# Cross-attention and expert kernel: the softmax probabilities transposed by DMA in f16 halves

## The reference

```
xn      = layernorm(x)
q, k, v = xn @ Wq.T, ctx @ Wk.T, ctx @ Wv.T          (16 heads of 64)
weights = softmax(q k^T / sqrt(128) + bias)          (128 x 120 for each head)
x       = x + (weights @ v) @ Wp.T
y       = layernorm(x)
x       = x + expert_ffn(y)                          (8 experts, top-32 tokens each in 128)
```

## Time and profile before

| | |
|---|---|
| time, median of 3 runs | 1197.02 us (1196.4 to 1198.01) |
| span of the profiled execution | 1194.1 us; the median lies 2.9 us above it |
| PE busy, by the page | 1133.8 us (95%) |
| ACT busy | 1010.4 us (85%) |
| DVE busy | 936.9 us (78%) |
| POOL busy | 663.5 us (56%) |
| attention stage | about 27 to 858 us of the span |
| PE, ACT, DVE, POOL busy from 451.7 to 464.5 us (one slot) | 12.80, 12.56, 11.37, 7.02 us |

### The profile page before, as it was taken

The page is one execution under the profiler, slowest core; times in us unless marked ns, Lnnn a source line. Parts: engine busy times, 40 slices in busy tenths (PEclk is TensorE's granted clock), DMA queues, the critical chain, the costliest instruction groups (busy, mean ns, idle before and its releaser), DMA issues. The chain is left out here.

```text
span 1194.1 us, 50330 instructions
## 1 busy us (share of the span) xinstructions
PE 1133.8 (95%) x15688; PEld 963.1 (81%) x15688; DVE 936.9 (78%) x3847; ACT 1010.4 (85%) x2919; POOL 663.5 (56%) x1149
## 2 busy tenths in 40 slices
PE   3999999999999999999999999999569999999996
PEld 3899999999999999999999999999436666666664
DVE  3888888888888888888888888888685665666553
ACT  3999999999999999999999999999447666666562
POOL 4555555555555555555555555554207767767673
PEclk9999999999999999999999999999869999999998
DMA  3000000000000000000000000000000111111112
GB/s 99 18 18 21 19 15 18 19 15 18 19 15 18 20 15 15 23 15 15 23 15 15 21 17 15 18 19 4 2 1 19 33 48 44 27 53 43 45 54 62
DMA packets 37002, 29.72 MB, mean 25 GB/s; under 512 B 13920, under 2 KB 30304, under 8 KB 36960
## 3 DMA queue, kind: packets, MB, share of 16 engines
q1 hardware_dynamic: 36096, 27.02, 8.6%
q10 hardware_dynamic: 864, 2.16, 0.5%
HBM read 16.58 MB, written 4.19 MB: 17 GB/s over the span
## 5 line engine op out<-in xcount | busy, mean ns | idle before, releaser
L383 ACT ACTIVATE probs<-neg,negmax 128x120 f32<-128x120 f32 x1024 | 322.9, 397 | 2.2 <-DVE negmax L412 0.6
L229 POOL TENSOR_TENSOR v_lo<-v_f,v_hi 120x256 f16<-120x256 f32 x256 | 167.9, 656 | 270.9 <-ACT v_hi L361 152.4
L412 DVE CUSTOM_DVE_ANT_0 neg<-bk_s,bias_sb 128x120 f32<-128x120 f32 x1024 | 228.4, 279 | 88.7 <-PE bk_s L536 80.0
L1101 POOL TENSOR_TENSOR hid<-hid_f,hid 128x512 f16<-128x512 f32 x128 | 167.6, 1313 | 73.7 <-ACT hid L1055 72.8
L422 DVE TENSOR_TENSOR qk_lo<-bk_a,qk_hi 128x496 f16<-128x496 f32 x256 | 171.5, 670 | 7.2 <-ACT qk_hi L346 7.2
L453 DVE TENSOR_TENSOR pT_lo<-bk_t,pT_hi 120x512 f16<-120x512 f32 x256 | 169.9, 664 | 0.3
L545 PE MATMUL bk_t<-ident,probs 128*120 128x128 f32 x1024 | 166.7, 285 | 1.6 <-ACT probs L383 1.6
L346 ACT CAST qk_hi<-bk_a 128x496 f16<-128x496 f32 x256 | 146.6, 572 | 24.6 <-PE bk_a L520 9.7
L375 ACT CAST pT_hi<-bk_t 120x512 f16<-120x512 f32 x256 | 157.5, 615 | 2.4 <-PE bk_t L545 2.4
L621 PE MATMUL bk_y<-wp_sb,oT 128*128 128x128 f32 x1024 | 156.2, 275 | 0.0
L1155 DVE TENSOR_TENSOR hid_f<-bk_u,silu 128x512 f32<-128x512 f32 x128 | 88.3, 690 | 85.4 <-ACT silu L1048 35.0
(11 more groups left out here) (168 smaller groups left out, 3981.7 us busy)
## 6 DMA issues: line engine op xcount, KB each, us to landing
y_all<-y SPq DMA_DIRECT2D x128, 64.0 KB, 2.0
wst<-ffn_w SPq DMA_DIRECT2D x64, 96.0 KB, 1.9
x_sb<-x SPq DMA_DIRECT2D x64, 64.0 KB, 1.8
out<-x_sb SPq DMA_DIRECT2D x16, 256.0 KB, 2.0
ctx_f<-ctx_t SPq DMA_DIRECT2D x64, 60.0 KB, 1.9
w_f<-wqkv_t ACTq DMA_DIRECT2D x3, 512.0 KB, 5.3
wp_sb<-wp_t ACTq DMA_DIRECT2D x1, 512.0 KB, 6.1
bias_sb<-bias ACTq DMA_DIRECT2D x1, 60.0 KB, 6.1
```

The costliest lines, as they stand in the source:

```text
L229: pool.tensor_tensor(v_lo[par][0:K, GH * g:GH * (g + 1), :], v_f[g % 2][0:K, :, :], v_hi[par][0:K, GH * g:GH * (g + 1), 0:DH], ALU.subtrac ...
L383: e = nc.scalar.activation(probs[g % 2][:, i, :], neg[g % 2][:, i, :], ACT.Exp, bias=negmax[g % 2][:, i:i + 1], scale=-1.0)
L412: r = nc.vector.tensor_tensor_reduce(out=neg[g % 2][:, i, :], in0=bk_s[i % 2][:, (i // 2) * K:(i // 2 + 1) * K], in1=bias_sb[:, :], scale= ...
L1101: nc.gpsimd.tensor_tensor(hid[1][par][:, ic, :], hid_f[ic % 2][:, :], hid[0][par][:, ic, :], ALU.subtract).then_inc(hid_lo_ready, 1)
```

## The change

PE makes no transposes of the probabilities any more. POOL casts the f32 probabilities (128 x 4 x 120) to their upper f16 half in the new buffer `p_parts` (128 columns for each head, the last 8 set to zero at the start), DVE subtracts it from the f32 probabilities to get the lower half, and SP issues a transposing DMA for each half, 128 x 512 f16 (128 KB), from SBUF to SBUF, into the new buffer `pT`. There are four buffers of each, one for each group of a slot. The casts of `pT_hi` on ACT and of `pT_lo` from PSUM on DVE go away, and so does the bank `bk_t`. PV runs four groups behind the scores (it was two), the output transposes five (three), the projection six (four). The residual add and its statistics move from step 3 of slot t (batch t-2) to step 1 (batch t-3), the second layernorm from batch t-3 to t-4, and one slot is added at the end (DRAIN 4). SP's three loads of a slot stand between the transposes, on two semaphores in place of one, and x and the context are loaded one slot earlier.

```diff
-DRAIN = 3
+DRAIN = 4
+PV_LAG = 4
+TURN_LAG = PV_LAG + 1
+PROJ_LAG = PV_LAG + 2
...
 @block.sync
+            def turn(t, g):
+                n = 4 * (t - 1) + g
+                for part, ready in ((0, p_hi_ready), (1, p_lo_ready)):
+                    sp.wait_ge(ready, n + 1)
+                    alone(sp)
+                    if part == 0 and some(n - GROUPS + 1):
+                        sp.wait_ge(pv_written, n - GROUPS + 1)
+                        alone(sp)
+                    sp.dma_start_transpose(pT[g][:, part * GH:(part + 1) * GH, :],
+                                           p_parts[g][:, part, :, :].rearrange("p b c -> p (b c)")
+                                           ).then_inc(pT_moved[g], 16)
             def slot(t, par):
...
+                if live(t - 1):
+                    turn(t, 0)
+                if live(t + 2):
+                    load_x(t + 2, par)
+                if live(t - 1):
+                    turn(t, 1)
+                if live(t + 1):
+                    load_ffn(t + 1, (par + 1) % 2)
+                if live(t - 1):
+                    turn(t, 2)
+                    turn(t, 3)
...
 @block.gpsimd
+            for i in range(GROUPS):
+                pool.memset(p_parts[i][:, :, :, K:], 0.0).then_inc(const_ready, 1)
...
+            def upper_parts(t, g):
+                if live(t - 1):
+                    n = 4 * (t - 1) + g
+                    pool.wait_ge(probs_ready, n + 1)
+                    if some(t - 1):
+                        pool.wait_ge(pT_moved[g], 32 * (t - 1))
+                    alone(pool)
+                    pool.tensor_copy(p_parts[g][:, 0, :, 0:K], probs[g % 2][:, :, :]).then_inc(p_hi_ready, 1)
...
+                upper_parts(t - 1, GROUPS - 1)
                 values(t - 1, GROUPS - 1, i)
...
                     pool.tensor_scalar(wsc[:, :], wst[par][:, :], WSCALE, None, ALU.mult).then_inc(pool_chain, 1)
+                upper_parts(t, 0)
                 values(t, 0, par)
...
+                upper_parts(t, 1)
                 values(t, 1, par)
...
+                upper_parts(t, 2)
                 values(t, 2, par)
...
 @block.scalar
-                b1, g1 = behind(t, g, 1)
-                if live(b1):
-
-                    act.wait_ge(pT_written, 4 * b1 + g1 + 1)
-                    if some(4 * b1 + g1 - 1):
-                        act.wait_ge(pv_written, 4 * b1 + g1 - 1)
-                    nc.scalar.copy(pT_hi[g1 % 2][0:K, :, :].rearrange("p a b -> p (a b)"),
-                                   bk_t[0:K, :]).then_inc(pT_hi_ready, 1)
...
 @block.vector
-                    dve.wait_ge(pT_hi_ready, 4 * b1 + g1 + 1)
-                    if some(4 * b1 + g1 - 1):
-                        dve.wait_ge(pv_written, 4 * b1 + g1 - 1)
-                    nc.vector.tensor_tensor(pT_lo[g1 % 2][0:K, :, :].rearrange("p a b -> p (a b)"), bk_t[0:K, :],
-                                            pT_hi[g1 % 2][0:K, :, :].rearrange("p a b -> p (a b)"),
-                                            ALU.subtract).then_inc(pT_lo_ready, 1)
+                    dve.wait_ge(p_hi_ready, 4 * b1 + g1 + 1)
+                    nc.vector.tensor_tensor(p_parts[g1][:, 1, :, 0:K], probs[g1 % 2][:, :, :],
+                                            p_parts[g1][:, 0, :, 0:K], ALU.subtract).then_inc(p_lo_ready, 1)
...
-                if g == GROUPS - 1 and live(t - 2):
-
-                    dve.wait_ge(proj_written, 4 * (t - 2) + 4)
-                    nc.vector.tensor_tensor(x_sb[:, t - 2, :], x_sb[:, t - 2, :], bk_y[:, 0:D],
+                if g == (PROJ_LAG + 3) % GROUPS and live(t - 3):
+
+                    dve.wait_ge(proj_written, 4 * (t - 3) + 4)
+                    nc.vector.tensor_tensor(x_sb[:, t - 3, :], x_sb[:, t - 3, :], bk_y[:, 0:D],
                                             ALU.add).then_inc(x1_ready, 1)
...
 @block.tensor
-                b1, g1 = behind(t, g, 1)
-                if live(b1):
-                    pe.wait_ge(probs_ready, 4 * b1 + g1 + 1)
-                    if some(4 * b1 + g1):
-                        pe.wait_ge(pT_lo_ready, 4 * b1 + g1)
-                    for i in range(GH):
-                        m = nc.tensor.transpose(bk_t[0:K, i * S:(i + 1) * S], probs[g1 % 2][:, i, :], ident[:, :])
-                    m.then_inc(pT_written, 1)
-                b2, g2 = behind(t, g, 2)
+                b2, g2 = behind(t, g, PV_LAG)
                 if live(b2):
 
-                    p2 = (par + 1) % 2 if g >= 2 else par
-                    pe.wait_ge(pT_lo_ready, 4 * b2 + g2 + 1)
+                    p2 = par
+                    pe.wait_ge(pT_moved[g2], 32 * (b2 + 1))
```

More of the change, by code:

```diff
@@ L118, in attention @@
         probs = two("probs", [S, GH, K], F32)
-        pT_hi = two("pT_hi", [128, GH, S], F16)
-        pT_lo = two("pT_lo", [128, GH, S], F16)
+        p_parts = [sb(f"p_parts{i}", [S, 2, GH, 128], F16) for i in range(GROUPS)]
+        pT = [sb(f"pT{i}", [128, 2 * GH, S], F16) for i in range(GROUPS)]
         rsum = sb("rsum", [S, GH], F32)
@@ L205, in _, with load_x, load_ffn @@
-            slots(sp, slot, end=B, first=0)
+            def load_x(b, par):
+                if some(b):
+                    sp.wait_ge(loaded_xc, 32 * b)
+                    alone(sp)
+                sp.dma_start(x_sb[:, b, :], x[:, b, :]).then_inc(loaded_xc, 16)
+                if some(b - 1):
+                    sp.wait_ge(ctx_ready, b - 1)
+                    alone(sp)
+                sp.dma_start(ctx_f[par][:, :], ctx_t[:, b, :]).then_inc(loaded_xc, 16)
+            def load_ffn(b, par):
+                if some(b):
+                    sp.wait_ge(loaded_ffn, 16 * b)
+                if some(b - 1):
+                    sp.wait_ge(ffnw_ready, b - 1)
+                alone(sp)
+                src = ffn_w[:, bass.ds(b * WCH, WCH)] if not isinstance(b, int) else ffn_w[:, b * WCH:(b + 1) * WCH]
+                sp.dma_start(wst[par][:, :], src).then_inc(loaded_ffn, 16)
@@ new lines, in slot @@
+            def slot(t, par):
+                if live(t - 1):
[9 more added lines that the diff above has]
+                    turn(t, 3)
+            load_x(0, 0)
+            slots(sp, slot, end=B + 1, loop_end=loop_end - 2)
@@ L300, in before @@
                     return each * (t - lag) if not isinstance(t, int) else each * min(max(t - lag, 0), B)
-                c = 1 + (t + 1) + before(-1, 2) + before(0, 2) + before(3, 1)
+                c = 1 + (t + 1) + before(-1, 2) + before(0, 2) + before(4, 1)
                 out = [c + 1]
-                for batch in (t + 1, t, t + 1, t, t - 3):
+                for batch in (t + 1, t, t + 1, t, t - 4):
                     out.append(out[-1] + (1 if live(batch) else 0))
@@ L346, in step @@
                     nc.scalar.copy(qk_hi[pw][:, gw, :], bk_a[:, 0:QK]).then_inc(qk_hi_ready, 1)
-                if gw == GROUPS - 1 and live(tw - 3):
-                    act.wait_ge(logits_written, tw - 2)
+                if gw == GROUPS - 1 and live(tw - 4):
+                    act.wait_ge(logits_written, tw - 3)
                     if live(tw):
                         act.wait_ge(v_written, 4 * tw + gw + 1)
-                    nc.scalar.copy(logits[:, tw - 3, :], bk_b[:, 256:256 + E]).then_inc(logits_ready, 1)
+                    nc.scalar.copy(logits[:, tw - 4, :], bk_b[:, 256:256 + E]).then_inc(logits_ready, 1)
                 if live(tw):
@@ L588, in step @@
                             pe.wait_ge(xT_ready, t + 2)
-                        if live(t - 3) and some(t - 2):
-                            pe.wait_ge(x2T_ready, t - 2)
+                        if live(t - 4) and some(t - 3):
+                            pe.wait_ge(x2T_ready, t - 3)
                     if g == 2:
@@ L593, in step @@
                             pe.wait_ge(xT_ready, t + 1)
[L594 to L595 removed]
+                        if live(t - 4) and some(t - 4):
+                            pe.wait_ge(x2T_ready, t - 4)
                         if live(t + 1):
```

101 lines of the change are left out of this document (46 added, 55 removed).

## The result

The changed kernel takes 1275.03 us (median of 4 runs, 1273.72 to 1276.05), against 1197.46 us for the kernel before in the same rounds: a ratio of 1.0646, 95% interval 1.0631 to 1.0661. That is 77.6 us slower; 1308 was forecast, 1203 to 1365 the range. Span against span it is 1274.2 - 1194.1 = 80.1 us. The granted clock is 1.00 from 200 to 700 us in both.

A forecast was written before the change was run, and what follows sets the result against it. The prediction took the ring PE, ACT, PE through `bk_b` as the bound; residual add 15, stall 92 and end 4 made 111 us, added to the 1194.1 span plus 2.9 for 1308 us, range 1203 to 1365.

The forecast's parts named there:

- The bound of before: Steady attention slots: PE waits for ACT's `v_hi` in a ring PE, ACT, PE through `bk_b`, 3.07 us a step.
- The rival that PE bounds: All steps: PE's work is the bound, so removing transposes saves 1.0 us a slot, 1135 us; chance 0.06.
- The moved residual add: DVE, step 1: add and statistics bring 0.67 us, exceeding ring and slack by 0.24 us a slot, 15 us in all.
- the stall: DVE's lower half in step 1, held by POOL's late cast and SBUF collisions: 1.46 us a slot, 92 us in all.
- The cast's 0.58: POOL's cast of the upper half, 480 columns: 0.58 us, extrapolated from casts of 120 and 192 columns.
- the low end: Step 1 with no SBUF collision: DVE waits only for POOL's late cast, 0.5 us a slot, 32 us; chance 0.22.
- `vpe`: POOL, step 0: held 0.42 us by DVE's lower half, making everything behind it on POOL, group 0's cast included, 0.42 later.
- The collision with `v_lo`: Step 1: POOL starts `v_lo` about 0.1 before DVE's lower half and holds DVE for its 0.66 us.
- The signs named: Changed profile: `neg` to `neg` of step 1 about 5.1 us, slot 14.6, lower half late or near 1.3, `vpe` over 0.22.
- 4 us for the end: Last batch two groups later: between 0 and two full steps of 3.07 us, taken as 4 us.
- The DMAs hidden: Eight transposing DMAs a slot, by bytes 1.3 us each against 1.6 allowed, cost 0; latency has 8 us or more.
- the rival's 5.2 us each: Transposing DMAs bound: by one skill figure 5.2 us each, 42 us a slot, near 3060 us; chance of transposes binding 0.19.

## Why the prediction was right, and where a size was off

- **The bound of before** held. Thinning the transposes out changed nothing and brought the wait for `v_hi` into the open. The rival that PE bounds (1135) is out.
- **The moved residual add, 0.24 us a slot.** With the cast first, step 1 is 3.63 us (forecast 3.64) and the slot 13.21, 0.33 over before. Steps 1 and 2 together give 0.21 of it, close to the forecast 0.24; the other 0.12 is in step 0 and was in no term. Putting the add back won 0.30 in the changed kernel, where the stall was left.
- **The cast's 0.58** is 0.585, and its place behind `wsc` gives the 0.50 of the low end.
- **The term that was mis-sized is the stall: 1.46 forecast, 0.97 measured**, 0.49 too much in 63 slots, 31 us of the 33 by which 1308 was high. The smaller errors nearly cancel: 7 us for step 0 and 2.5 for the end were missing; against them, 5 us of the stall did not reach the slot (0.88 of 0.97 us did), and the first `neg` came 2.3 us earlier. The part that failed is `vpe`: it was to be held 0.42 and pass all of it on. It was held (0.46 in place of 0.22 us), but 0.24 only, and since `neg` of step 1 comes 0.14 later behind `vpe` than before (1.00 us against 0.86), the cast was about 0.1 later and not 0.42. The value "1.04 without `vpe`", which the text gave beside it, was within 0.07 of what came. The collision with `v_lo` was as described.
- **The signs named** came, smaller: from `neg` to `neg` of step 1 4.47 us and not 5.1, a slot of 14.09 and not 14.6, the lower half behind POOL's cast and 1.10 long (1.3 was named), `vpe` 0.46 long, PE idle 0.26 us before the queries and keys of step 2, released by `qk_lo`.
- **4 us for the end** were 6.5, above the bound of 6.1, and not by later PV alone. With one DMA a group the end is only 2.0 us longer than before; the other 4.4 us go with SP's queue, PE's waits for the last two groups and the slower clock after them. That 4 came near is partly luck.
- **The DMAs hidden**: yes, in the slots, with landings of 2.4 us; the rival's 5.2 us each did not come. The worry was the right resource at the wrong place: not the engines' throughput, but SP's issuing. An issue takes 1.20 of the 1.6 us that the text allowed; with the loads and the gaps SP needs 13.19 us a slot. That fits into 14.09 us, but not into the 12.9 of before, so the sum was also lucky here: "0" held only because the kernel had become slow enough. It bounded as soon as the stall was repaired. Nothing in the trace of before showed this price.

What stays open: why step 0 is 0.12 us longer. With two value banks it is 3.04 us, so it hangs on the ring through `bk_b`, but no run shows which part of the ring grew. A version with the cast first, two value banks and the residual add out of step 1 at once was not tried; as built here it needs one bank more than the one set free.

## To carry over

Work taken from an engine that is busy 95% of the time gives nothing if that engine waits in a ring; look for a distance between starts that never changes. What takes its place goes to other engines' in-order lists, and there its position counts more than its length: the same 0.58 us cast, two instructions earlier on POOL, was worth 52 us. And a queue that issues transfers is an engine too: count what one issue holds it for, times the issues of a period, and use few and large ones. If that sum is over the period, the queue falls behind until the slack of several steps is used up, and a trace then shows waits far from where the work was made: match each wait with its own transfer.

## What the runs showed of the hardware

- A transposing DMA from SBUF to SBUF holds SP 1.20 us for 128 KB and 1.23 for 256 KB; a plain load holds it 0.33 to 0.36. It lands after 2.4 and 3.1 us, against 1.9 to 2.0 for plain loads of 60 to 96 KB.
- A VectorE operation with a single full-size SBUF input can stand still beside POOL as well: `xn`, f32 tensor_scalar of 128 x 128, took 0.73 us in place of 0.33 with `v_lo` begun at the same time. The Trainium skill (SBUF — State Buffer, "SBUF: two separate sides") counts VectorE operations in a two-port performance mode among those that contend with GpSimd, beside those with two SBUF inputs. The wait agrees with that if `xn` runs in such a mode, which no trace here names.
- By the same section the first to start holds the other for its whole length. Not all of it is seen here: the lower half began at 454.75, 0.37 after `wsc` (which ran until 455.09), and took its 0.63 undisturbed. In the other order, in the kernel with the cast first and two value banks, `wsc` began 0.16 after a lower half, at 462.96, and took 1.03 us in place of 0.71. And in the changed kernel `vpe` came 0.25 after a lower half that ran 0.38 more, and was held 0.24, not to its end plus its own length.
